# Weighed values through a buffer: VectorE scales them in one product, GpSimd adds them to x

## The chip, the cores and the metric

One core of a Trainium2 chip runs the kernel. The time is that of the device, in microseconds (us), the median of the runs. The engines run side by side and meet through semaphores: TensorE (PE; its weight loads PEld), VectorE (DVE), ScalarE (ACT), GpSimd (POOL), and SyncE (SP), which issues the transfers. Each engine works its own instructions in the order in which they were written.

## The reference, cut to what matters

x has 8 sequences of 512 tokens of 128 numbers. It goes through a routed feed-forward layer, an attention with 16 heads, and the same feed-forward layer again; each adds to x. The change lies in the attention alone:

```python
s = jnp.einsum('bihd,bjhd->bhij', qr, jnp.conj(kr)).real
maha = jnp.maximum(qn[..., None] + (E * E)[None] * kn[:, :, None, :] - 2.0 * E[None] * s, 0.0) / V[None]
logits = coef * jnp.log1p(maha / nu[None, :, None, None]) - 0.5 * DH_ * jnp.log(V)[None]
logits = jnp.where(causal[None, None], logits, -jnp.inf)
A = jax.nn.softmax(logits, axis=-1)
out = jnp.einsum('bhij,bjhd->bihd', A.astype(v.dtype), v)
y = jnp.concatenate([out.real.reshape(B_, N_, DKt), out.imag.reshape(B_, N_, DKt)], axis=-1)
return y @ Wo          # and x = x + this
```

E is a decay exp(-mu |t - t'|) of each head, V depends on it, qn and kn are the squared norms of queries and keys. The kernel multiplies the values by Wo beforehand, so that each head and sequence adds a matrix of 512 tokens by 128 numbers straight to x.

## The kernel before

x stays in SBUF for the whole run (`x_sb`, 128 partitions, 32 tiles of 128x128; a sequence has four). The first feed-forward layer ends near 260 us, the attention near 1476, the second feed-forward layer at the end.

The attention makes 128 pairs of a head and a sequence, in one long row of steps. Head h takes the eight sequences, then head h + 1. The values of two heads are projected together, under the first of the two, which is called even: `values` runs in eight steps (an even octet) and not in the next eight (an odd octet). `PAIRS` is 128, `i` counts pairs of heads and `r` the step in it.

In a step for pair r the engines work on several pairs at once:

- TensorE, in this order: the scores of pair r into the PSUM tile `pS` (L1191), norms of r + 1 (L1204, L82), the projection of r + 2 into `pQK` (L72 to L74), the turn of the probabilities of r - 1 in `pS` (L1233), under even heads the values of r, and `weigh` of r - 2: the probabilities times the values into the PSUM tile `p7` (L1311).
- VectorE: `peaks` of r - 1 (L1578: logarithm plus table, both in SBUF, and the minimum of each row, four pieces of 128, 384, 512 and 256 columns), half of `accumulate` of r - 3 (L1609), `distances` of r (L1587 and the two decay products L1591, out of `pS`), the transpose of the query norms of r + 1 (L1597), the other half of `accumulate`, the rotation's sine and cosine products of r + 2 out of `pQK` (L1631, L1633), the reciprocal of the row sums of r - 1 (L1601). In some steps under even heads it builds the next heads' tables (L1537 to L1567) ahead of the next peaks.
- ScalarE: the exponentials of r - 1 (`soften`, L1376), key norms, clamps, the copy of the turned probabilities, logarithms, squares, and under even heads the values out of PSUM.
- GpSimd: `rotate` of r + 1 (L1500), four products `ek` of decay and key norms (L1509), the query norms `qnorm` (L1517).
- SP: two transfers of the sine product of r + 2, whose halves change places (`crossed`); rotate waits for them.

`accumulate` makes, for each of the four tiles of a sequence, x = p7 * rinv + x, where rinv is the reciprocal of the row sums. Its last product signals `acc_done`; the next `weigh` waits for that before it writes into `p7`. For the last head's eight sequences `moments` follows on VectorE: it waits for `acc_done` and takes mean and variance of the new x (L1618, L1622) for the second feed-forward layer. This is in steps 123 to 130, and the last steps have more work of that layer's head between (variance, refinement, routing).

Of the kernel before, what the change touches and what calls it, by code (L numbers as in the profile page):

```python
# [24 lines left out]
ALU = mybir.AluOpType  # L25
# [3 lines left out]
P = 128  # L29
D = 128  # L30
B, N = 8, 512
TILES = N // P
# [15 lines left out]
SW = 1280  # L48
# [9 lines left out]
def wait(eng, sem, value):  # L58

    if not (isinstance(value, int) and value <= 0):  # L60
        eng.wait_ge(sem, value)
# [981 lines left out]
def attention_phase(nc, s):  # L1043
# [4 lines left out]
    with ExitStack() as ctx:  # L1048
        sb = lambda name, shape, dt=F32: ctx.enter_context(nc.sbuf_tensor(name, shape, dt))
# [7 lines left out]
        decay2, wqk_raw, by_cos, by_sin, crossed = s.decay2, s.wqk_raw, s.by_cos, s.by_sin, s.crossed  # L1057
        squares, rot, knorm, u, z = s.squares, s.rot, s.knorm, s.u, s.z
        qnorm = sb("qnorm", [P, 2, TILES])
        q_turned = sb("q_turned", [P, 2, P])  # L1060
        ek = sb("ek", [P, SW])
        probT = [sb(f"probT{k}", [P, SW]) for k in range(2)]

# [4 lines left out]
        rinv = sb("rinv", [P, 4, TILES])  # L1068
        stats = sb("stats_at", [P, TILES, 6])
        S = s.S  # L1070
# [18 lines left out]
        def hp(h, k):  # L1089

            return s.params[:, h, k:k + 1]
# [16 lines left out]
        def live(i, r):  # L1108

            return not isinstance(i, int) or 0 <= i * 16 + r < PAIRS  # L1110

        def parity(r):

            return (r // B) % 2

        def values_made(i, r):

            return i * B + (r // 16) * B + (r % B + 1 if parity(r) == 0 else B)
# [66 lines left out]
        def _(pe):  # L1185
# [114 lines left out]
            def weigh(i, r):  # L1300
                n = i * 16 + r
                if n == 0:
                    pe.wait_ge(S["late_lo"], 2)
                wait(pe, S["trc_done"], n + 1)
                wait(pe, S["acc_done"], n)
                wait(pe, S["val_done"], values_made(i, r))
                val = val_even[r % B % 3] if parity(r) == 0 else val_odd[r % B]
                turned = probT[r % 2]
                for I in range(TILES):
                    for J in range(I + 1):  # L1310
                        last = pe.matmul(s.p7[:, I * P:(I + 1) * P], turned[:, OFF[I] + J * P:OFF[I] + (J + 1) * P],  # L1311
                                         val[:, J * P:(J + 1) * P], start=(J == 0), stop=(J == I))
                last.then_inc(S["av_done"], 1)
# [175 lines left out]
        def _(g):  # L1489
# [22 lines left out]
            def query_norms(i, r):  # L1512
                n, h = i * 16 + r, i * 2 + r // B
                wait(g, S["qt_done"], n + 1)
                wait(g, S["relu_done"], 2 * (n - 1))
                column = q_turned[:, r % 2].rearrange("p (c d) -> p c d", c=TILES)[:, :, 0]
                g.tensor_scalar(qnorm[:, r % 2, :], column, hp(h, NEG_NU_A), None, ALU.subtract).then_inc(S["qn_done"], 1)  # L1517

            def a_step(i, r):
                if live(i, r + 1):  # L1520
                    if (i, r) != (0, -1):
                        rotate(i, r + 1)
                    spread(i, r + 1)
                    query_norms(i, r + 1)
                if i == 0 and r == -1:
                    build_first()

# [3 lines left out]
        def _(v):  # L1531
# [68 lines left out]
                v.wait_ge(S["exp_done"], i * 16 + r + 1)  # L1600
                v.reciprocal(rinv[:, r % 4, :], rsum[:, r % 4, :]).then_inc(S["rinv_done"], 1)  # L1601

            def accumulate(i, r, tiles=range(TILES)):
                n, b = i * 16 + r, r % B
                v.wait_ge(S["av_done"], n + 1)
                v.wait_ge(S["rinv_done"], n + 1)
                for I in tiles:
                    xt = s.x_sb[:, b * TILES + I, :]
                    last = v.scalar_tensor_tensor(xt, s.p7[:, I * P:(I + 1) * P], rinv[:, r % 4, I:I + 1], xt,  # L1609
                                                  ALU.mult, ALU.add)  # L1610
                if TILES - 1 in tiles:
                    last.then_inc(S["acc_done"], 1)

            def moments(r, n):
                b = r % B
# [117 lines left out]
            def a_step(i, r):  # L1733
                n = i * 16 + r
                if n == PAIRS:
                    accumulate(i, r - 3)
                if live(i, r - 1):
                    peaks(i, r - 1)
                if i == 0 and r in (1, 2):
                    late_low(r - 1)  # L1740
                if live(i, r):
                    if live(i, r - 3):
                        accumulate(i, r - 3, range(TILES // 2))
                    distances(i, r)
                if n == PAIRS - 1:
                    head_low(0)
                    head_low(1)
                if live(i, r + 1):
                    query_norms(i, r + 1)
                if live(i, r - 3) and n != PAIRS:  # L1750
                    accumulate(i, r - 3, range(TILES // 2 if live(i, r) else 0, TILES))
                if n == PAIRS:
                    head_gap()
                    head_first()
# [35 lines left out]
def program(nc, args, out):  # L1790
    with ExitStack() as ctx:
        sb = lambda name, shape, dt=F32: ctx.enter_context(nc.sbuf_tensor(name, shape, dt))
        ps = lambda name, shape: ctx.enter_context(nc.psum_tensor(name, shape, F32))
        s = Shared(args, out)
# [21 lines left out]
        def part(n):  # L1816
# [12 lines left out]
        names = ("w_in trig_in0 trig_in1 w_hi w_lo hp_done arg_done decay_done decay2_done lnv_done lam0_done "  # L1829
                 "lam_done qk_done bs_done crossed_in cos_done sq_done rot_done norm_done q2_done qn_done kn_done "  # L1830
                 "ek_done s_done w_done t_done relu_done ln_done zred_done exp_done v_done "
                 "qt_done val_done tr_done trc_done av_done rinv_done acc_done stat_done dve_passed pool_passed sp_passed "
                 "late_stat late_mv late_var late_ln late_root late_rstd late_step late_xn late_xt late_hi late_lo mv_done expanded0 expanded1")
        s.S = {n: ctx.enter_context(nc.semaphore(n)) for n in names.split()}
        names = ("guw_done silu_done var_done ln_done root_done rstd_done xn_dve xt_done xhi_done xlo_done "
# [12 lines left out]
        s.silu1 = part(2 * N).rearrange("p (a t) -> p a t", a=2)  # L1848
        dense_phase(nc, s, 0)
        attention_phase(nc, s)  # L1850
        dense_phase(nc, s, 1)

# [46 lines left out]
```

## Time and profile before

| | |
|---|---|
| median of 3 runs | 1686.73 us (1685.27 to 1687.78) |
| the profiled execution | 1685.38 us, span 1683.6 |
| PE busy | 1624.1 us, 96% |
| DVE busy | 1494.5 us, 89% |
| ACT busy | 1443.1 us, 86% |
| POOL busy | 1013.6 us, 60% |
| granted TensorE clock | 0.999 |

The span runs from the first to the last instruction that the profile shows. Busy shares are over the whole span, and so mix the three phases. In rows of the timeline, the first number is the start in us from the span's start, the second the duration in us; xN at the end says how many instructions were merged into the row, and a bracket names idle time before it and what ended it. Successive instructions of VectorE overlap by some 0.07 us in these rows, so what one costs is read from start to start.

### The profile page before, as it was taken

Reading aid. Unit: us, or ns where it says so; the run is one execution under the profiler, and the core shown is the slowest. Engines: PE = TensorE matmul, PEld = TensorE weight load, DVE = VectorE, ACT = ScalarE, POOL = GpSimd, SP = SyncE. Lnnn points to the kernel's source line nnn. Section 1 sums busy time; section 2 is a strip of 40 time slices with the busy share of each in tenths; the row PEclk is TensorE's granted clock in tenths of the full one; section 3 lists DMA queues with packets and bytes.
Section 4 is the critical chain, followed back from the end, with each engine's and each line's share of the span. In section 5 each row is a group of like instructions: output and inputs, shape, how many; then the busy total and the mean of one; then the engine's idle time right before and its main releaser. Section 6 shows DMA issues by size and latency. Waiting matters only on the chain. (4 is left out here: it accounts for less than half of the span.)

```text
span 1683.6 us, 31247 instructions
## 1 busy us (share of the span) xinstructions
PE 1624.1 (96%) x9690; PEld 1227.8 (73%) x9690; DVE 1494.5 (89%) x3380; ACT 1443.1 (86%) x2909; POOL 1013.6 (60%) x954
## 2 busy tenths in 40 slices
PE   5999988999999999999999999999999999899998
PEld 4787865777776777677777777777776776677876
DVE  6878878999999999999999999999999989977665
ACT  6677678999999999999999999999999998765765
POOL 3564556666666666665766666666666656245555
PEclk9999999999999999999999999999999999999999
DMA  6000022232223323232222323232232322100000
GB/s 178 1 1 1 1 97 73 64 92 64 76 70 76 79 64 85 58 82 70 75 74 64 92 64 76 55 92 69 74 84 60 80 59 51 26 8 7 13 13 13
DMA packets 50484, 100.05 MB, mean 59 GB/s; under 512 B 8208, under 2 KB 25872, under 8 KB 50320
## 3 DMA queue, kind: packets, MB, share of 16 engines
q1 hardware_dynamic: 50320, 98.07, 22.7%
q8 instruction: 78, 1.28, 0.3%
q14 instruction: 86, 0.70, 0.1%
HBM read 17.95 MB, written 5.24 MB: 14 GB/s over the span
## 5 line engine op out<-in xcount | busy, mean ns | idle before, releaser
L1500 POOL TENSOR_TENSOR early<-early 128x1024 f32<-128x1024 f32 x127 | 303.7, 2391 | 421.4 <-PE pS L1191 227.6
L661 POOL TENSOR_TENSOR hid_lo_d<-hid_d,hid_hi_d 128x512 fp32r<-128x512 f32 x176 | 231.4, 1315 | 218.4 <-ACT hid_hi_d L566 211.8
L1392 ACT ACTIVATE early<-early,qnorm 128x128 f32<-128x128 f32 (+3 forms) x512 | 246.6, 552 | 68.0 <-DVE early L1591 67.3
L1191 PE MATMUL pS<-early 128*128 128x128 f32 (+3 forms) x1024 | 297.6, 433 | 0.4 <-PEq L115 0.4
L1376 ACT ACTIVATE early<-early,nmax 128x128 f32<-128x128 f32 (+3 forms) x512 | 280.9, 558 | 7.7 <-DVE nmax L1578 7.4
L1191 PEld LDWEIGHTS pS<-early 128*128 128x128 f32 x1024 | 164.7, 191 | 96.1 <-issue 61.4
L1587 DVE SCALAR_TENSOR_TENSOR pS<-pS,ek 128x1280 f32<-128x1280 f32 x128 | 190.9, 1492 | 43.5 <-PE pS L1191 41.9
L1509 POOL TENSOR_TENSOR ek<-early 128x128 f32<-128x128 f32 (+3 forms) x256 | 216.1, 877 | 3.0 <-ACT early L1384 2.6
L1509 POOL TENSOR_TENSOR ek<-decay,early 128x128 f32<-128x128 f32 (+3 forms) x256 | 215.0, 873 | 0.0
L1233 PE MATMUL pS<-ident,early 128*128 128x128 f32 x1280 | 184.9, 278 | 13.3 <-DVE early L1591 7.0
L1405 ACT ACTIVATE early<-early,params 128x512 f32<-128x512 f32 (+1 forms) x256 | 196.4, 816 | 0.0
L1233 PEld LDWEIGHTS pS<-ident,early 128*128 128x128 f32 x1280 | 143.5, 141 | 62.1 <-DVE early L1591 32.1
L566 ACT ACTIVATE hid_hi_d<-hid_d 128x512 fp32r<-128x512 f32 x176 | 111.1, 631 | 60.8 <-DVE hid_d L794 43.0
L1399 ACT ACTIVATE probT<-pS 128x1280 f32<-128x1280 f32 x128 | 155.9, 1218 | 3.4 <-PE pS L1233 3.4
L1311 PE MATMUL p<-val_odd,probT 128*128 128x128 f32 x1280 | 156.9, 278 | 1.3 <-ACT probT L1399 1.3
L1311 PE MATMUL p<-val_even,probT 128*128 128x128 f32 x1280 | 154.4, 276 | 0.0
L1311 PEld LDWEIGHTS p<-val_odd,probT 128*128 128x128 f32 x1280 | 147.9, 192 | 6.0 <-ACT probT L1399 1.6
L1609 DVE SCALAR_TENSOR_TENSOR x_sb<-p,rinv,x_sb 128x128 f32<-128x128 f32 x512 | 149.4, 332 | 1.3 <-PE p L1311 1.3
L1311 PEld LDWEIGHTS p<-val_even,probT 128*128 128x128 f32 x1280 | 148.1, 192 | 1.5
L1578 DVE CUSTOM_DVE_ANT_0 early<-early,lam,params 128x128 f32<-128x128 f32 (+3 forms) x256 | 133.6, 575 | 8.8 <-issue 0.5
L1204 PE MATMUL pV<-early,ones 128*128 128x512 f32 x254 | 131.1, 598 | 4.4 <-ACT val_odd L1418 3.9
L1411 ACT ACTIVATE early<-pQK 128x1024 f32<-128x1024 f32 x127 | 127.6, 1005 | 1.8 <-DVE early L1633 1.8
(393 smaller groups left out, 3752.5 us busy)
## 6 DMA issues: line engine op xcount, KB each, us to landing
early<-early SPq DMA_DIRECT2D x263, 256.0 KB, 3.4
early<-trig_d SPq DMA_DIRECT2D x64, 64.0 KB, 2.0
trig_d<-early SPq DMA_DIRECT2D x3, 1024.0 KB, 6.9
early<-in_w SPq DMA_DIRECT2D x3, 704.0 KB, 8.7
x_sb<-in_x SPq DMA_DIRECT2D x4, 512.0 KB, 8.3
early<-in_wqk SPq DMA_DIRECT2D x16, 128.0 KB, 3.4
cos<-trig_d SPq DMA_DIRECT2D x32, 64.0 KB, 2.2
sin<-trig_d SPq DMA_DIRECT2D x32, 64.0 KB, 2.0
```

The lines of the kernel that those rows point to most:

```text
L661: g.tensor_tensor(hid_lo[:, par], hid[:, par], hid_hi[:, par].bitcast(F32), ALU.subtract).then_inc(lo_done, 1)
L1191: last = pe.matmul(s.pS[:, span(I)], rot[:, I * P:(I + 1) * P], rot[:, N:N + (I + 1) * P], start=True, stop=True)
L1233: last = pe.transpose(s.pS[:, col:col + P], z[:, col:col + P], s.ident[:])
L1311: last = pe.matmul(s.p7[:, I * P:(I + 1) * P], turned[:, OFF[I] + J * P:OFF[I] + (J + 1) * P], val[:, J * P:(J + 1) * P], start=(J == 0), ...
L1376: last = a.activation(z[:, span(I)], z[:, span(I)], ACT.Exp, bias=nmax[:, I:I + 1], scale=-1.0, accum_out=rsum[:, r % 4, I:I + 1])
L1392: last = a.activation(u[:, span(I)], u[:, span(I)], ACT.Relu, bias=qnorm[:, r % 2, I:I + 1])
L1399: a.activation(probT[r % 2][:], s.pS[:, 0:SW], ACT.Copy).then_inc(S["trc_done"], 1)
L1405: a.activation(u[:, half], u[:, half], ACT.Ln, bias=hp(h, U_MIN)).then_inc(S["ln_done"], 1)
L1500: g.tensor_tensor(rot[:], by_cos[:], crossed[:], ALU.add).then_inc(S["rot_done"], 1)
L1509: last = g.tensor_tensor(ek[:, span(I)], decay[par][:, span(I)], knorm[:, 0:(I + 1) * P], ALU.mult)
L1587: v.scalar_tensor_tensor(s.pS[:, 0:SW], s.pS[:, 0:SW], -2.0, ek[:], ALU.mult, ALU.add).then_inc(S["w_done"], 1)
L1609: last = v.scalar_tensor_tensor(xt, s.p7[:, I * P:(I + 1) * P], rinv[:, r % 4, I:I + 1], xt, ALU.mult, ALU.add)
```

## The change

VectorE now scales all four tiles in one product into a new buffer `weighed`, and signals `y_done`; GpSimd adds the buffer to x as the last thing in its step, and signals `acc_done`. `weigh` waits for `y_done`. There is one buffer, so the product waits for the add of the pair before. Under odd heads (and where no values are made) the product stands ahead of the transpose of the query norms, under even heads behind it; no part of it is left ahead of `distances`. `moments` waits for `acc_done` as before. The transposed query norms move into columns of `dist` that nothing else uses by then, to make room for the buffer.

```diff
@@ -1057,7 +1057,8 @@
         decay2, wqk_raw, by_cos, by_sin, crossed = s.decay2, s.wqk_raw, s.by_cos, s.by_sin, s.crossed
         squares, rot, knorm, u, z = s.squares, s.rot, s.knorm, s.u, s.z
         qnorm = sb("qnorm", [P, 2, TILES])
-        q_turned = sb("q_turned", [P, 2, P])
+        q_turned = s.dist[:, 2 * N:SW].rearrange("p (k d) -> p k d", k=2)
+        weighed = sb("weighed", [P, TILES, P])
         ek = sb("ek", [P, SW])
         probT = [sb(f"probT{k}", [P, SW]) for k in range(2)]
 
@@ -1302,7 +1303,7 @@
                 if n == 0:
                     pe.wait_ge(S["late_lo"], 2)
                 wait(pe, S["trc_done"], n + 1)
-                wait(pe, S["acc_done"], n)
+                wait(pe, S["y_done"], n)
                 wait(pe, S["val_done"], values_made(i, r))
                 val = val_even[r % B % 3] if parity(r) == 0 else val_odd[r % B]
                 turned = probT[r % 2]
@@ -1516,12 +1517,20 @@
                 column = q_turned[:, r % 2].rearrange("p (c d) -> p c d", c=TILES)[:, :, 0]
                 g.tensor_scalar(qnorm[:, r % 2, :], column, hp(h, NEG_NU_A), None, ALU.subtract).then_inc(S["qn_done"], 1)
 
+            def accumulate(i, r):
+                n, b = i * 16 + r, r % B
+                g.wait_ge(S["y_done"], n + 1)
+                xb = s.x_sb[:, b * TILES:(b + 1) * TILES, :]
+                g.tensor_tensor(xb, xb, weighed[:], ALU.add).then_inc(S["acc_done"], 1)
+
             def a_step(i, r):
                 if live(i, r + 1):
                     if (i, r) != (0, -1):
                         rotate(i, r + 1)
                     spread(i, r + 1)
                     query_norms(i, r + 1)
+                if live(i, r - 3):
+                    accumulate(i, r - 3)
                 if i == 0 and r == -1:
                     build_first()
 
@@ -1600,16 +1609,13 @@
                 v.wait_ge(S["exp_done"], i * 16 + r + 1)
                 v.reciprocal(rinv[:, r % 4, :], rsum[:, r % 4, :]).then_inc(S["rinv_done"], 1)
 
-            def accumulate(i, r, tiles=range(TILES)):
-                n, b = i * 16 + r, r % B
+            def normalise_out(i, r):
+                n = i * 16 + r
                 v.wait_ge(S["av_done"], n + 1)
                 v.wait_ge(S["rinv_done"], n + 1)
-                for I in tiles:
-                    xt = s.x_sb[:, b * TILES + I, :]
-                    last = v.scalar_tensor_tensor(xt, s.p7[:, I * P:(I + 1) * P], rinv[:, r % 4, I:I + 1], xt,
-                                                  ALU.mult, ALU.add)
-                if TILES - 1 in tiles:
-                    last.then_inc(S["acc_done"], 1)
+                wait(v, S["acc_done"], n)
+                v.tensor_tensor(weighed[:], s.p7.rearrange("p (c d) -> p c d", c=TILES),
+                                rinv[:, r % 4, :].unsqueeze(2).broadcast_to([P, TILES, P]), ALU.mult).then_inc(S["y_done"], 1)
 
             def moments(r, n):
                 b = r % B
@@ -1733,22 +1739,23 @@
             def a_step(i, r):
                 n = i * 16 + r
                 if n == PAIRS:
-                    accumulate(i, r - 3)
+                    normalise_out(i, r - 3)
                 if live(i, r - 1):
                     peaks(i, r - 1)
                 if i == 0 and r in (1, 2):
                     late_low(r - 1)
                 if live(i, r):
-                    if live(i, r - 3):
-                        accumulate(i, r - 3, range(TILES // 2))
                     distances(i, r)
                 if n == PAIRS - 1:
                     head_low(0)
                     head_low(1)
-                if live(i, r + 1):
+                values_next = live(i, r) and parity(r) == 0
+                if live(i, r + 1) and values_next:
                     query_norms(i, r + 1)
                 if live(i, r - 3) and n != PAIRS:
-                    accumulate(i, r - 3, range(TILES // 2 if live(i, r) else 0, TILES))
+                    normalise_out(i, r - 3)
+                if live(i, r + 1) and not values_next:
+                    query_norms(i, r + 1)
                 if n == PAIRS:
                     head_gap()
                     head_first()
@@ -1829,7 +1836,7 @@
         names = ("w_in trig_in0 trig_in1 w_hi w_lo hp_done arg_done decay_done decay2_done lnv_done lam0_done "
                  "lam_done qk_done bs_done crossed_in cos_done sq_done rot_done norm_done q2_done qn_done kn_done "
                  "ek_done s_done w_done t_done relu_done ln_done zred_done exp_done v_done "
-                 "qt_done val_done tr_done trc_done av_done rinv_done acc_done stat_done dve_passed pool_passed sp_passed "
+                 "y_done qt_done val_done tr_done trc_done av_done rinv_done acc_done stat_done dve_passed pool_passed sp_passed "
                  "late_stat late_mv late_var late_ln late_root late_rstd late_step late_xn late_xt late_hi late_lo mv_done expanded0 expanded1")
         s.S = {n: ctx.enter_context(nc.semaphore(n)) for n in names.split()}
         names = ("guw_done silu_done var_done ln_done root_done rstd_done xn_dve xt_done xhi_done xlo_done "
```

## Rows read from the trace of the kernel before

**Rows 1.** Busy us by stretch, six even octets: summed length, then engines.

```profile
sum 473.38, PE 472.35 PEld 365.11 DVE 438.14 ACT 452.57 POOL 288.63; mean PE 78.73 PEld 60.85 DVE 73.02 ACT 75.43 POOL 48.10
```

**Rows 2.** Timeline of PE and DVE: scores and L1587, even, then odd.

```profile
728.19 2.32 PE L1191 MATMUL pS<-early 128*128 128x128 f32 x8
...
730.56 1.50 DVE L1587 SCALAR_TENSOR_TENSOR pS<-pS,ek 128x1280 f32<-128x1280 f32 x1 [0.93 <-PE pS L1191]
...
822.63 2.32 PE L1191 MATMUL pS<-early 128*128 128x128 f32 x8
```

**Rows 3.** Busy times by stretch: seven odd octets, sum.

```profile
sum 494.09, PE 487.01 PEld 347.97 DVE 483.89 ACT 456.58 POOL 338.21; mean PE 69.57 PEld 49.71 DVE 69.13 ACT 65.23 POOL 48.32
```

**Rows 4.** Timeline of DVE: one undisturbed step under an odd head.

```profile
816.44 1.48 DVE L1587 SCALAR_TENSOR_TENSOR pS<-pS,ek 128x1280 f32<-128x1280 f32 x1
817.96 1.55 DVE L1591 TENSOR_TENSOR early<-pS,decay 128x512 f32<-128x512 f32 x2
819.43 0.30 DVE L1597 STREAM_TRANSPOSE q_turned<-pV 128x128 f32<-128x128 f32 x1
819.66 0.57 DVE L1609 SCALAR_TENSOR_TENSOR x_sb<-p,rinv,x_sb 128x128 f32<-128x128 f32 x2
820.14 1.21 DVE L1631 TENSOR_TENSOR early<-pQK,sin 128x1024 f32<-128x1024 f32 x1
...
822.71 0.35 DVE L1578 CUSTOM_DVE_ANT_0 early<-early,lam,params 128x128 f32<-128x128 f32 x1
...
822.99 0.61 DVE L1578 CUSTOM_DVE_ANT_0 early<-early,lam,params 128x384 f32<-128x384 f32 x1
...
824.61 0.60 DVE L1609 SCALAR_TENSOR_TENSOR x_sb<-p,rinv,x_sb 128x128 f32<-128x128 f32 x2
825.13 1.49 DVE L1587 SCALAR_TENSOR_TENSOR pS<-pS,ek 128x1280 f32<-128x1280 f32 x1
```

**Rows 5.** Timeline of POOL and DVE: a first piece of peaks beside ek.

```profile
962.33 1.98 POOL L1509 TENSOR_TENSOR ek<-decay,early 128x512 f32<-128x512 f32 x2
...
963.78 0.67 DVE L1578 CUSTOM_DVE_ANT_0 early<-early,lam,params 128x128 f32<-128x128 f32 x1
...
964.38 0.61 DVE L1578 CUSTOM_DVE_ANT_0 early<-early,lam,params 128x384 f32<-128x384 f32 x1
```

**Rows 6.** DVE and POOL: a second piece of peaks beside ek, qnorm.

```profile
813.83 1.07 DVE L1578 CUSTOM_DVE_ANT_0 early<-early,lam,params 128x384 f32<-128x384 f32 x1
...
814.48 0.59 POOL L1517 TENSOR_SCALAR qnorm<-q_turned,params 128x4 f32<-128x4 f32 x1
```

**Rows 7.** Timeline of POOL: first and last row of an even step.

```profile
730.70 2.38 POOL L1500 TENSOR_TENSOR early<-early 128x1024 f32<-128x1024 f32 x1 [3.87 <-PE pS L1191]
...
736.38 0.30 POOL L1517 TENSOR_SCALAR qnorm<-q_turned,params 128x4 f32<-128x4 f32 x1
```

**Rows 8.** Line L1631: least, median, greatest duration in ns; first and last start.

```profile
L1631 DVE TENSOR_TENSOR early<-pQK,sin x64: 1189/1211/1216, 325.2 to 1439.3; 128x1024 f32<-128x1024 f32 x64
```

**Rows 9.** Groups by line, POOL; behind the count: busy us, mean ns, idle us.

```profile
L661 POOL TENSOR_TENSOR hid_lo_d<-hid_d,hid_hi_d 128x512 fp32r<-128x512 f32 x176 | 231.4, 1315 | 218.4 <-ACT hid_hi_d L566 211.8 <-PE p L74 4.3 <-PE pV L74 2.2
```

**Rows 10.** Timeline of DVE: L1587 starting an even octet's last step.

```profile
779.88 1.50 DVE L1587 SCALAR_TENSOR_TENSOR pS<-pS,ek 128x1280 f32<-128x1280 f32 x1 [0.26 <-PE pS L1191]
```

**Rows 11.** Timeline of DVE and POOL: the tail, steps 123, 124 and 128.

```profile
1418.55 0.87 DVE L1618 BATCH_NORM_STATS2 stats_at<-x_sb 128x6 f32<-128x128 f32 x4
...
1419.75 1.19 DVE L1631 TENSOR_TENSOR early<-pQK,sin 128x1024 f32<-128x1024 f32 x1
...
1421.01 0.29 POOL L1517 TENSOR_SCALAR qnorm<-q_turned,params 128x4 f32<-128x4 f32 x1
...
1424.46 1.49 DVE L1587 SCALAR_TENSOR_TENSOR pS<-pS,ek 128x1280 f32<-128x1280 f32 x1
...
1425.31 2.38 POOL L1500 TENSOR_TENSOR early<-early 128x1024 f32<-128x1024 f32 x1 [4.01 <-DMA early<-early]
...
1462.74 1.13 DVE L1609 SCALAR_TENSOR_TENSOR x_sb<-p,rinv,x_sb 128x128 f32<-128x128 f32 x4 [1.34 <-PE p L1311]
```

## The prediction

> **What bounds the kernel now.** I read the busy shares of the page first (TensorE 96%, VectorE 89%, ScalarE 86%, GpSimd 60%): three engines close together, so an average decides nothing. Then I cut the attention phase at the starts of the decay's first product (L1587) into octets of eight steps. A step is one sequence under one head; octets alternate, because `values` runs only under even heads.
>
> Even octets: six take 473.38 us, 9.86 a step, and TensorE is busy for 472.35 of it [rows 1]. VectorE's L1587 starts where the score products end (728.19 + 2.32 = 730.51, start 730.56), after 0.93 of idling [rows 2]. TensorE bounds them.
>
> Odd octets: seven take 494.09, 8.82 a step, VectorE busy for 483.89 [rows 3]. In the timeline of an undisturbed odd step VectorE's instructions stand end to end from one L1587 to the next, 816.44 to 825.13 = 8.69 [rows 4]. The scores end at 822.63 + 2.32 = 824.95 [rows 2]. So VectorE bounds odd steps, with TensorE's floor only 0.13 below (824.95 + 0.05 - 816.44 = 8.56). The other 0.13 of the mean comes from steps in which VectorE is disturbed.
>
> On that disturbance this forecast stands. `peaks` (L1578) reads two SBUF tensors. Its 128x128 form takes 0.35, but 0.67 at 963.78, where GpSimd's ek products still run to 962.33 + 1.98 = 964.31; the next piece starts at 964.38, 0.07 after that end [rows 4, 5]. Its 128x384 form takes 0.61, but 1.07 at 813.83, and GpSimd's 4-element qnorm beside it takes 0.59 instead of 0.30 [rows 4, 6, 7]. Peaks and GpSimd's products keep each other waiting, in both directions. L1631, with one operand in PSUM, shows nothing of the kind: 1189 to 1216 ns over 64 [rows 8].
>
> **VectorE's part of the change.** Removed: four products of 128x128 from PSUM, two before L1587 (825.13 - 824.61 = 0.52) and two behind the transpose (820.14 - 819.66 = 0.48): 1.00 a step [rows 4]. Added: one product of 512 columns out of PSUM. The L1591 pair covers 1280 columns in 819.43 - 817.96 = 1.47, so 512 cost 0.59; the upper end is 0.69, a start of 0.10 included. I take 0.60, as the neighbours overlap so: 0.40 less a step. Peaks start 0.12 later (6.39 behind L1587 instead of 822.71 - 816.44 = 6.27), and nothing stands between them and the next L1587. Alone this makes VectorE's odd step 8.29, and TensorE would hold it at 8.56. The new wait on `acc_done` ahead of the product asks for the add of one step earlier, long done. `weigh` now waits for `y_done`: with the product ahead of the transpose in odd steps that comes at 3.6, earlier than the last accumulate before (3.7), so it costs nothing.
>
> **GpSimd's part.** One add of 128x512 from two SBUF tensors. The same shape takes 1.315 elsewhere [rows 9]; I take 1.31. It is queued last, behind rotate, the four ek products and qnorm. These start 0.14 after L1587 (730.70 - 730.56) and end at 736.38 + 0.30 = 736.68, 6.12 after it [rows 2, 7]. So the add runs from 6.12 to 7.43, in idle time of GpSimd's queue: nothing behind it waits. But peaks want to start at 6.39. They find the add running; the second piece starts 0.07 after its end, at 7.50, and the rest takes 824.61 - 822.99 = 1.62 [rows 4, 5]: VectorE is free at 9.12. The bounds of this collision: nothing at all (8.56 a step, a gain), and the add falling between two pieces, so that its whole 1.31 and some 0.2 of handover come on top of 6.39 + 1.90: 9.8.
>
> The copy that feeds rotate moves too: where rotate waits for it, it starts 5.56 behind the sine product (1419.75 to 1425.31) [rows 11]. That product goes from 3.70 (820.14 - 816.44) to 3.82, so the copy lands at 9.38. With a step of T, rotate starts 9.38 - T behind the next L1587, and T = (9.38 - T) + 8.98 gives T = 9.18. As some copies come later (an estimate, from the odd mean's 0.13 over the undisturbed step), I take 9.25. There are 59 odd steps before the tail: 59 x (9.25 - 8.82) = **+25 us**.
>
> The Trainium skill, "SBUF — State Buffer", section "Who interferes with whom", says that a VectorE instruction with two SBUF inputs and a GpSimd instruction that reads SBUF lock each other out for the whole instruction. Taken to the letter, the next piece could start only 0.28 after the GpSimd product's end; the row at 963.78 shows 0.07. By the rule the odd step would be 0.2 longer (the last rival).
>
> Even steps: VectorE has the same collision (7.50 - 6.39 - 0.28 = 0.83 for peaks, up to 1.1 where a table product stands first; I take 1.0). It loses 0.12 and gains 0.52 ahead of L1587. Where it idled 0.9, all this is hidden under TensorE. In the last two steps of an octet VectorE also builds tables and idled 0.26 or less [rows 10]: 0.26 + 0.40 - 1.0 = -0.34 in each. Seven octets: **+4 us** (0 to 10).
>
> **The tail.** In steps 123 to 126 `moments` waits for `acc_done`, which GpSimd now gives. The sine and cosine products, the reciprocal and peaks are queued behind it on VectorE. Moments began at 1418.55; GpSimd's own work of that step ends at 1421.01 + 0.29, and the add with 0.07 for its signal brings 1422.68: 4.13 later [rows 11]. Less the 0.40 saved, and some 0.4 because rotate starts at 0.2 instead of 0.6 after a step of 9.2: +3.3. The late sine product then delays the next rotate (it needs 5.56, and 1424.46 - 1419.75 - 0.52 = 4.19 are left to the next L1587), to 1.4: +4.5 for each of the next two. In the fourth the refinement steps hide this again: +3.3. Together 15.6. In the last four sequences the add follows the product at once: 1.4 of waiting each, against 0.5 saved (four products took 1.13 [rows 11]): +3.4. **+19 us** (10 to 23).
>
> **Sum.** 25 + 4 + 19 = 48. The profiled execution took 1685.4 (span 1683.6 and 1.8 around it), 1.3 under the median of 1686.73. So 1733.4 as profiled, and 1735 as the median.
>
> **Rivals.**
> Port yields: peaks, issued back to back, keep going and the add waits until they are done (qnorm's 0.59 speaks for it, the 1.07 beside it against [rows 6]). It is decided by who goes first at 6.4. Odd steps fall to TensorE's 8.56: 59 x -0.26 = -15, even 0, tail +19: 1690; with the tail's low end 1681. Not slower, at best faster.
> Half block: the add has its operands early and peaks lose only 0.5: odd steps stay at 8.8, even 0, tail 19: 1706. The 0.67 at 963.78, over nearly all of a product's rest, speaks against it.
> Between the pieces: where rotate starts later than 0.27 behind L1587, a peaks piece goes first and the add falls behind it: 9.8 a step, +58, even 8, tail 19: 1771 if in every step. The 1.07 at 813.83 is such a case [rows 6]; a longer step pulls rotate forward again, which speaks against every step.
> Full block: the first piece starts only at the add's end, 0.2 later in 59 odd steps: +12, 1747. The 0.07 speaks against it.
>
> **Chances.** Forecast 0.57 (its own range 1722 to 1748); port yields 0.10; half block 0.11; between the pieces 0.12; full block 0.10. The range 1698 to 1764 leaves out the first rival and the upper part of the third. Some 0.2% (3.4 us) can be told from no change. Faster 0.04 and the same 0.06 both come from the first rival; slower 0.90.
>
> **What would show it.** In the profile after: odd octets near 74 us, even ones near 79; the first piece of peaks near 1.2 instead of 0.35 in most steps, ending with the add; VectorE still without idle time in odd steps, TensorE with some ahead of its turns; the add at 1.3; ahead of the moments 3 to 5 us of VectorE's idle time in four steps, released by GpSimd. Wrong, if peaks keep 0.35 while the add runs, if the new product takes more than 0.7, or if odd octets lie under 70 us.

## The result and the profile after

The changed kernel takes 1731.97 us (median of 4 runs, 1731.3 to 1736.96) against 1686.0 (4 runs, 1684.09 to 1687.78): 1.028 of before, interval 1.0257 to 1.0302. It is slower. Its profiled execution took 1731.3 us, span 1729.5, at a granted clock of 0.993.

The page of the kernel after: span, then busy time of each engine with its share and count.

```profile
span 1729.5 us, 30866 instructions
...
PE 1634.8 (95%) x9690; PEld 1228.5 (71%) x9690; DVE 1551.7 (90%) x2996; ACT 1455.0 (84%) x2909; POOL 1176.1 (68%) x1082
```

VectorE was given 0.4 us less to do in each of 128 steps, and is busy for 57 us more. The groups by line, shapes apart, say where (behind the bar: busy us, mean ns of one, then idle time before and its releaser):

```profile
L1617 DVE TENSOR_TENSOR weighed<-p,rinv 128x512 f32<-128x512 f32 x128 | 85.5, 668 | 1.5 <-PE p L1312 1.5
L1587 DVE CUSTOM_DVE_ANT_0 early<-early,lam,params 128x128 f32<-128x128 f32 x64 | 57.4, 898 | 4.6 <-ACT early L1406 0.6 <-issue 0.4
...
L1524 POOL TENSOR_TENSOR x_sb<-x_sb,weighed 128x512 f32<-128x512 f32 x128 | 167.7, 1310 | 24.5 <-DVE weighed L1617 24.5
```

The new product and the new add cost what they should. Under odd heads the first piece of peaks (now L1587) takes 898 ns on average, where an undisturbed one takes 0.35 us [rows 4]. All pieces of peaks together grew from 287.8 to 349.8 us.

Cut at the starts of the decay's first product (now L1596), as before, the sums of seven odd and of six even octets:

```profile
sum 513.29, PE 488.39 PEld 344.14 DVE 505.93 ACT 464.85 POOL 405.94; mean PE 69.77 PEld 49.16 DVE 72.28 ACT 66.41 POOL 57.99
...
sum 480.08, PE 476.65 PEld 365.51 DVE 468.03 ACT 454.77 POOL 352.98; mean PE 79.44 PEld 60.92 DVE 78.00 ACT 75.79 POOL 58.83
```

They answer to [rows 3] and [rows 1]: seven odd octets 19.2 us longer, six even ones 6.7. VectorE's timeline of one odd step (the answer to [rows 4]), and GpSimd's of the same step:

```profile
831.21 1.49 DVE L1596 SCALAR_TENSOR_TENSOR pS<-pS,ek 128x1280 f32<-128x1280 f32 x1
832.74 1.56 DVE L1600 TENSOR_TENSOR early<-pS,decay 128x512 f32<-128x512 f32 x2
834.21 0.68 DVE L1617 TENSOR_TENSOR weighed<-p,rinv 128x512 f32<-128x512 f32 x1
834.81 0.31 DVE L1606 STREAM_TRANSPOSE dist<-pV 128x128 f32<-128x128 f32 x1
...
837.50 1.23 DVE L1587 CUSTOM_DVE_ANT_0 early<-early,lam,params 128x128 f32<-128x128 f32 x1
...
838.65 0.61 DVE L1587 CUSTOM_DVE_ANT_0 early<-early,lam,params 128x384 f32<-128x384 f32 x1
...
840.27 1.49 DVE L1596 SCALAR_TENSOR_TENSOR pS<-pS,ek 128x1280 f32<-128x1280 f32 x1
```

```profile
831.36 2.40 POOL L1501 TENSOR_TENSOR early<-early 128x1024 f32<-128x1024 f32 x1 [1.03 <-DMA early<-early]
833.71 3.36 POOL L1510 TENSOR_TENSOR ek<-decay,early 128x128 f32<-128x128 f32 x4
837.04 0.30 POOL L1518 TENSOR_SCALAR qnorm<-dist,params 128x4 f32<-128x4 f32 x1
837.30 1.27 POOL L1524 TENSOR_TENSOR x_sb<-x_sb,weighed 128x512 f32<-128x512 f32 x1
```

Read the two side by side. The add starts at 837.30, the first piece of peaks 0.20 later, and the add runs to 838.57. The piece is shown as busy until 838.73, 0.16 longer than the add (the rows of successive pieces overlap by 0.07 or 0.08), and the second one starts at 838.65, 0.08 behind the add's end. The step takes 840.27 - 831.21 = 9.06.

The tail, step 123: VectorE, GpSimd, and one later row of VectorE (the answers to [rows 11]).

```profile
1441.88 1.49 DVE L1596 SCALAR_TENSOR_TENSOR pS<-pS,ek 128x1280 f32<-128x1280 f32 x1
...
1449.67 0.87 DVE L1624 BATCH_NORM_STATS2 stats_at<-x_sb 128x6 f32<-128x128 f32 x4 [3.89 <-POOL x_sb L1524]
...
1455.07 1.49 DVE L1596 SCALAR_TENSOR_TENSOR pS<-pS,ek 128x1280 f32<-128x1280 f32 x1
...
1503.22 0.87 DVE L1624 BATCH_NORM_STATS2 stats_at<-x_sb 128x6 f32<-128x128 f32 x4 [1.39 <-POOL x_sb L1524]
```

```profile
1448.37 1.27 POOL L1524 TENSOR_TENSOR x_sb<-x_sb,weighed 128x512 f32<-128x512 f32 x1
1456.44 2.37 POOL L1501 TENSOR_TENSOR early<-early 128x1024 f32<-128x1024 f32 x1 [6.80 <-DMA early<-early]
```

VectorE stands idle for 3.89 us until GpSimd's queue has reached the add. The table of waits (total us, times, longest) shows what is new over the whole run; the second row is the exponentials of ScalarE waiting for peaks:

```profile
DVE stats_at L1624 <- POOL x_sb L1524: 20.7, 7, 4.7
...
ACT early L1377 <- DVE nmax L1587: 50.1, 78, 4.9
```

From the starts of the decay's first product in both traces, the 45.9 us of span (1683.6 to 1729.5) fall so: 59 odd steps +19.8 (8.83 to 9.17 each), 56 even steps +6.8 (9.86 to 9.98), steps 123 to 126 +14.7, everything behind the last decay product +4.0, the first eight steps +0.5.

### The profile page after: what moved, and what is told of

Same layout as the page of the kernel before. It is cut to its first block and busy times, and to the rows that moved or that the text cites. A ratio compares the mean times of both kernels' runs of the same rounds, so it can differ in the third digit from the quotient of the medians.

```text
span 1729.5 us, 30866 instructions
## 1 busy us (share of the span) xinstructions
PE 1634.8 (95%) x9690; PEld 1228.5 (71%) x9690; DVE 1551.7 (90%) x2996; ACT 1455.0 (84%) x2909; POOL 1176.1 (68%) x1082
## 5 line engine op out<-in xcount | busy, mean ns | idle before, releaser
L1596 DVE SCALAR_TENSOR_TENSOR pS<-pS,ek 128x1280 f32<-128x1280 f32 x128 | 191.2, 1494 | 17.1 <-PE pS L1192 16.0
L1587 DVE CUSTOM_DVE_ANT_0 early<-early,lam,params 128x128 f32<-128x128 f32 (+3 forms) x256 | 183.0, 767 | 4.6 <-ACT early L1406 0.6
L1524 POOL TENSOR_TENSOR x_sb<-x_sb,weighed 128x512 f32<-128x512 f32 x128 | 167.7, 1310 | 24.5 <-DVE weighed L1617 24.5
L1205 PE MATMUL pV<-early,ones 128*128 128x512 f32 x254 | 131.4, 599 | 15.4 <-ACT early L1412 7.0
```

The source lines that it names most:

```text
L1524: g.tensor_tensor(xb, xb, weighed[:], ALU.add).then_inc(S["acc_done"], 1)
L1587: last = v.tensor_tensor_reduce(z[:, span(I)], u[:, span(I)], lam(h)[:, near(I)], hp(h, NEG_COEF), HIGHEST, ALU.add, ALU.min, nmax[:, I:I ...
L1596: v.scalar_tensor_tensor(s.pS[:, 0:SW], s.pS[:, 0:SW], -2.0, ek[:], ALU.mult, ALU.add).then_inc(S["w_done"], 1)
```

## The experiments

Theory: two waits. Peaks, which read two SBUF tensors, and GpSimd's add, which reads two as well, keep each other waiting in every step; and moments wait for an add at the end of GpSimd's queue. The rivals put the cost on the new product, on its place, on the waits (`y_done`, `acc_done`) or on GpSimd's time as such. Each row below has the ratio of the kernel's runs to those of the kernel before, with its interval. The other columns are of the profiled execution and worked out from the starts of the decay's first product: mean of the 59 odd and the 56 even steps, and the length of steps 123 to 126 and of all behind the last, against before.

| kernel | ratio (interval) | odd | even | 123 to 126 | behind |
|---|---|---|---|---|---|
| before | 1 | 8.83 | 9.86 | 0 | 0 |
| after | 1.0279 (1.0257 to 1.0302) | 9.17 | 9.98 | +14.7 | +4.0 |
| no_add | 0.9886 (0.987 to 0.9903) | 8.59 | 9.86 | -1.9 | -1.1 |
| memset2 | 1.0009 (0.9999 to 1.0018) | 8.54 | 9.87 | +14.4 | +2.3 |
| half_add | 1.0068 (1.0053 to 1.0083) | 8.77 | 9.87 | +13.0 | +0.7 |
| between | 1.0138 (1.0122 to 1.0154) | 9.02 | 9.87 | +6.6 | +2.6 |
| tail_old | 1.0167 (1.015 to 1.0184) | 9.23 | 9.98 | 0.0 | +0.1 |
| even_only | 0.9995 (0.9986 to 1.0004) | 8.78 | 9.89 | +0.1 | 0.0 |
| sine_first | 1.0147 (1.0132 to 1.0162) | 9.18 | 9.90 | +1.6 | +0.1 |
| acc_behind | 1.0053 (1.004 to 1.0067) | 8.93 | 9.86 | +2.4 | 0.0 |
| one_ahead | 0.9984 (0.9975 to 0.9993) | 8.77 | 9.86 | +3.1 | 0.0 |

**no_add.** The product stays, GpSimd's add goes (cut from the diff):

```diff
-                wait(pe, S["y_done"], n)
+                wait(pe, S["acc_done"], n)
...
-                if live(i, r - 3):
-                    accumulate(i, r - 3)
...
-                                rinv[:, r % 4, :].unsqueeze(2).broadcast_to([P, TILES, P]), ALU.mult).then_inc(S["y_done"], 1)
+                                rinv[:, r % 4, :].unsqueeze(2).broadcast_to([P, TILES, P]), ALU.mult).then_inc(S["acc_done"], 1)
```

> GpSimd's add is left out (the attention's result is not added to x); VectorE's product signals acc_done itself. Theory (peaks and the add exclude each other, and moments wait for the add): odd steps fall from 9.17 to TensorE's 8.56, the first piece of peaks is back near 0.35, tail and even octets lose their excess: 1670 (1664 to 1678). Rival (VectorE's new product or its place costs the time): odd steps stay above 8.9, over 1700.

Measured: 1666.24 us, inside the range. Seven odd octets, and the first piece of peaks:

```profile
sum 480.61, PE 477.24 PEld 347.16 DVE 471.24 ACT 455.11 POOL 339.69; mean PE 68.18 PEld 49.59 DVE 67.32 ACT 65.02 POOL 48.53
```

```profile
L1585 DVE CUSTOM_DVE_ANT_0 early<-early,lam,params 128x128 f32<-128x128 f32 x64 | 32.9, 514 | 4.0 <-issue 0.4
```

VectorE's part alone would be worth 19.6 us of 1685.84. The whole loss, and more, comes with the add; the product, its place and the moved query norms are all still in this kernel. The piece's 514 instead of 410 ns before is what ek alone does to it in a shorter step.

**memset2.** The same place in GpSimd's queue and the same waits, but two fills of `weighed` that only write, in place of the add that reads:

```diff
-                g.tensor_tensor(xb, xb, weighed[:], ALU.add).then_inc(S["acc_done"], 1)
+                g.memset(weighed[:], 0.0).then_inc(S["set_done"], 1)
+                g.wait_ge(S["set_done"], n + 1)
+                g.memset(weighed[:], 0.0).then_inc(S["acc_done"], 1)
```

> In place of the add GpSimd writes zeros over the buffer, twice, one after the other (x gets nothing): it is busy at the same place of its queue and signals from there, but reads nothing. Theory (the two shut each other out over reads from SBUF): the first piece of peaks keeps 0.35 to 0.55 beside it, odd steps stay at the 8.6 measured without an add; the moments still wait for it: 1668 to 1690, by the length of the two writes. Rival (any work of GpSimd at that place, by its queue or by writing to SBUF, costs the 0.6 a step): odd steps 9.0 or more, 1710 to 1735.

Measured: 1687.13, by the theory. The fills, by line, and a step's timeline on VectorE and on GpSimd:

```profile
L1524 POOL MEMSET weighed<- 128x512 f32 x128 | 67.2, 525 | 23.6 <-DVE weighed L1619 23.6
```

```profile
796.79 0.61 DVE L1589 CUSTOM_DVE_ANT_0 early<-early,lam,params 128x384 f32<-128x384 f32 x1
...
797.33 0.74 DVE L1589 CUSTOM_DVE_ANT_0 early<-early,lam,params 128x512 f32<-128x512 f32 x1
```

```profile
796.97 0.52 POOL L1524 MEMSET weighed<- 128x512 f32 x1
797.55 0.53 POOL L1526 MEMSET weighed<- 128x512 f32 x1
```

Peaks run through the fills at their own 0.61 and 0.74. GpSimd is busy for 1.1 us of the end of the step all the same (525 + 560 ns), and odd steps take 8.54: neither GpSimd's time nor the waits, but its reading, makes odd steps long. The tail keeps +14.4: there it is the place in the queue alone. The two parts of the cost come apart, and the tail by itself eats what 59 odd steps save.

The Trainium skill, "SBUF — State Buffer", section "Who interferes with whom", says that a VectorE instruction with two SBUF inputs contends with a GpSimd instruction that reads SBUF, and not with one that only writes it. These rows agree: 1.23 for the piece beside the add, 0.61 and 0.74 beside the fills.

**half_add.** The add over two of the four tiles:

```diff
-                g.tensor_tensor(xb, xb, weighed[:], ALU.add).then_inc(S["acc_done"], 1)
+                g.tensor_tensor(xb[:, 0:2], xb[:, 0:2], weighed[:, 0:2], ALU.add).then_inc(S["acc_done"], 1)
```

> The add takes two of the four tiles (the other two are left out): 0.74 us instead of 1.31 by the ek product of 256 columns. Theory (peaks wait as long as the add has to go): odd steps 8.8 to 8.9, even octets without excess, tail 0.57 shorter in eight places: 1704 (1696 to 1712). Rival (a price of each meeting, whatever its length): odd steps 9.1, 1722 to 1730.

Measured: 1697.25, inside the range. The add takes 828 ns instead of 1310 (0.74 us had been expected), and odd steps take 8.77, which is 0.40 less for 0.48 less of reading; even steps are back at 9.87. The less GpSimd reads at that place, the less it costs.

**between.** The add of the pair before, with operands long there, in the middle of the four ek products:

```diff
                 for I in ORDER:
+                    if I == ORDER[2] and live(i, r - 4):
+                        accumulate(i, r - 4)
...
-                if live(i, r - 3):
+                if live(i, r - 3) and not live(i, r + 1):
                     accumulate(i, r - 3)
```

> The add is queued between the second and the third ek product instead of last; nothing else changes. Theory (GpSimd's 7.36 of reading and the 1.9 of peaks can't overlap, so that 9.2 a step is due wherever the add stands): odd steps 9.1 to 9.3 as before, now with ek and qnorm beside peaks; the moments wait 2.2 less in four steps: 1723 (1715 to 1732). Rival (the add only stands at the wrong place): odd steps 8.6 to 8.7, 1696 (1690 to 1702).

Measured: 1709.7, between the two expectations, so both were wrong. One odd step of that kernel, GpSimd and VectorE:

```profile
683.50 1.28 POOL L1526 TENSOR_TENSOR x_sb<-x_sb,weighed 128x512 f32<-128x512 f32 x1
684.74 2.02 POOL L1512 TENSOR_TENSOR ek<-decay,early 128x512 f32<-128x512 f32 x2
686.74 0.60 POOL L1520 TENSOR_SCALAR qnorm<-dist,params 128x4 f32<-128x4 f32 x1
```

```profile
685.82 0.36 DVE L1589 CUSTOM_DVE_ANT_0 early<-early,lam,params 128x128 f32<-128x128 f32 x1
...
686.11 1.07 DVE L1589 CUSTOM_DVE_ANT_0 early<-early,lam,params 128x384 f32<-128x384 f32 x1
```

With the add out of the way, the later ek products meet peaks. Here the first piece comes just behind the border of two ek products (684.74 + 1.01 = 685.75) and keeps its 0.36; only the second waits, for the last product. This step took 8.65; steps in which rotate had started over 1.5 us behind the decay product took 9.7 to 10.2. So place matters in part, and my sentence that the step is 9.2 wherever the add stands does not hold. The tail's excess falls from 14.7 to 6.6, since the add no longer comes last.

**tail_old.** From step 123 on VectorE accumulates as before; all else as after. (Some 30 lines choose the way by the step's number; core:)

```diff
+            def new_way(i, r):
+                # of the step in which the pair's values are added
+                n = i * 16 + r
+                return n < (H - 1) * B + 3
...
+                    if new:
+                        normalise_out(i, r - 3)
+                    else:
+                        accumulate(i, r - 3, range(TILES // 2 if live(i, r) else 0, TILES))
```

> The last eight pairs, those with moments, are added by VectorE as before the change; all others go through the buffer. Theory: the excess of the tail (14.7 in steps 123 to 126 and 4.0 behind them) goes, all else stays: 1713 (1710 to 1717). Rival (the tail is only where a delay from before comes out): 1726 or more.

Measured: 1714.12, inside the range. The tail is back to within 0.1 us and no wait of VectorE for GpSimd's add is left, while odd steps stay long, at 9.23. So the two waits come apart: 1731.97 - 1714.12 = 17.9 us go with the tail and what is behind it, where the traces had 14.7 + 4.0 = 18.7. (In the two traces the odd steps differ as well, 9.17 and 9.23, or 3.8 us over 59; why was not looked into.)

**even_only.** The same switch, the new way only in steps r = 0 to 4 under even heads (37 adds in the trace, two of them in the first octet):

```diff
+                return n < (H - 1) * B + 3 and parity(r) == 0 and r % B < 5
```

> Only steps 0 to 4 of the even octets go through the buffer, all others as before. Theory (there the collision is the same, 0.8 on VectorE, and hidden under TensorE's 9.86): 1686 (1684 to 1690), with pieces of peaks stretched in these steps. Rival (each add costs, wherever it is): 35 adds at 0.36, the mean price of an add (46 us for 128), 1698.

Measured: 1685.45, no change. A collision in such a step: the third piece of peaks takes 1.75 instead of 0.74, and VectorE still idles 0.57 ahead of the decay's first product (L1609 in this kernel).

```profile
566.31 1.75 DVE L1600 CUSTOM_DVE_ANT_0 early<-early,params 128x512 f32<-128x512 f32 x1
...
569.04 1.50 DVE L1609 SCALAR_TENSOR_TENSOR pS<-pS,ek 128x1280 f32<-128x1280 f32 x1 [0.57 <-PE pS L1200]
```

Where TensorE bounds the step and VectorE idles ahead of that product, the collision is nearly free: in the trace the 56 even steps are 1.4 us longer in all, which the odd steps, 2.9 us shorter here, cover in the total.

The last three kernels go back to the one before and ask whether the gain that no_add shows can be had without GpSimd.

**sine_first.** In odd steps the sine product goes ahead of the transpose, and all four accumulate products ahead of `distances`:

```diff
-                        accumulate(i, r - 3, range(TILES // 2))
+                        accumulate(i, r - 3, range(TILES if early else TILES // 2))
                     distances(i, r)
...
+                if early:
+                    turn_sine(i, r + 2)
...
-                if live(i, r - 3) and n != PAIRS:
+                if live(i, r - 3) and n != PAIRS and not early:
```

> The kernel before the change, but in odd steps VectorE makes the sine product straight behind distances, and all four accumulate products ahead of them; GpSimd adds nothing. If it is the late start of rotate that brings ek beside peaks, rotate starts 0.7 earlier, at 0.14 in most steps, and odd steps come to their undisturbed 8.69 to 8.72: 59 x -0.12 = -7, 1679 (1676 to 1682). Rival (the 0.13 of the mean has another cause, or TensorE waits for the later transpose or distances): 1686 or more.

Measured: 1710.21, a miss by 31 us. The collisions are gone, as meant: the first piece takes 0.35 in odd steps. But the step is 9.22. VectorE and ScalarE in one:

```profile
829.34 1.49 DVE L1587 SCALAR_TENSOR_TENSOR pS<-pS,ek 128x1280 f32<-128x1280 f32 x1
...
835.62 0.35 DVE L1578 CUSTOM_DVE_ANT_0 early<-early,lam,params 128x128 f32<-128x128 f32 x1 [0.66 <-ACT early L1405]
...
838.55 1.49 DVE L1587 SCALAR_TENSOR_TENSOR pS<-pS,ek 128x1280 f32<-128x1280 f32 x1
```

```profile
833.48 1.22 ACT L1399 ACTIVATE probT<-pS 128x1280 f32<-128x1280 f32 x1
834.60 1.54 ACT L1405 ACTIVATE early<-early,params 128x512 f32<-128x512 f32 x2
```

Peaks wait 0.66 for ScalarE's logarithms and start 6.28 behind L1587. In [rows 4] they start 6.27 behind it, although VectorE had other work ahead of them there. In the kernel after it is 6.29, with again other work ahead. Two more rows of the step of [rows 4], VectorE's last one ahead of peaks and ScalarE's logarithms:

```profile
822.41 0.17 DVE L1601 RECIPROCAL rinv<-rsum 128x4 f32<-128x4 f32 x1
```

```profile
821.69 1.53 ACT L1405 ACTIVATE early<-early,params 128x512 f32<-128x512 f32 x2
```

Peaks start 0.13 behind the end of the reciprocal there, where successive instructions of VectorE otherwise overlap, and 822.71 - 821.69 = 1.02 behind the start of the logarithms; in sine_first it is 835.62 - 834.60 = 1.02 as well. So they waited for the logarithms before the change too, only too briefly to stand out. A loop over two engines was hidden in those rows: decay products, clamps, the copy of the turned probabilities, logarithms (6.28 to the start of peaks), and peaks themselves (837.51 - 835.62 = 1.89 for the four pieces): 8.17 at least. Every product between peaks and L1587 comes on top: two (0.52) gave 8.69, four (1.04) give 9.21. "VectorE's instructions end to end" was the wrong reading; the length agreed.

**acc_behind.** With the loop in mind: nothing between peaks and L1587, all four products behind `distances`, ahead of the sine product:

```diff
-                    if live(i, r - 3):
+                    if live(i, r - 3) and not early:
                         accumulate(i, r - 3, range(TILES // 2))
...
+                if early:
+                    accumulate(i, r - 3)
+                    turn_sine(i, r + 2)
...
-                if live(i, r - 3) and n != PAIRS:
+                if live(i, r - 3) and n != PAIRS and not early:
```

> The kernel before the change, but in odd steps all four accumulate products stand straight behind distances, and the sine product behind them; GpSimd adds nothing. In sine_first, peaks waited 0.66 for the logarithms: from L1587 over decay products, clamps, copy and logarithms to peaks and the next L1587 runs a second loop, of 8.17 without accumulate, and whatever stands between peaks and L1587 is added to it (0.52 gave 8.69, 1.04 gave 9.21). If so, odd steps are no longer held by it but by TensorE's 8.45 or VectorE's sum of 8.55; with some ek beside peaks, as rotate starts 0.25 later, 8.60 to 8.70: 59 x -0.17 = -10, 1676 (1672 to 1680). Rival (8.69 is VectorE's own sum, or weigh waits for the later acc_done): 1685 or more.

Measured: 1695.26; the rival held. VectorE's and TensorE's rows of one odd step:

```profile
829.48 1.50 DVE L1587 SCALAR_TENSOR_TENSOR pS<-pS,ek 128x1280 f32<-128x1280 f32 x1 [0.36 <-PE pS L1191]
...
832.49 1.12 DVE L1609 SCALAR_TENSOR_TENSOR x_sb<-p,rinv,x_sb 128x128 f32<-128x128 f32 x4
```

```profile
833.71 2.47 PE L1311 MATMUL p<-val_odd,probT 128*128 128x128 f32 x20 [0.21 <-issue]
836.01 2.32 PE L1191 MATMUL pS<-early 128*128 128x128 f32 x8
```

`weigh` starts 0.10 behind the end of the last product (833.61), after 0.21 of standing still: it waits for `acc_done`. That closes another loop: 4.13 from L1587 to the end of the last product, 0.10 to `weigh`, 4.62 to the end of the scores (836.01 + 2.32 = 838.33), and 0.05 to the next L1587 as in [rows 2], 8.90 in all. 44 of the 59 odd steps take 8.88 or 8.89. (The one shown takes 9.09, because a piece of peaks is stretched in it.) Here the changed kernel's one product, 0.60 instead of 1.0 long, helps: in no_add most odd steps take 8.45 or 8.46.

**one_ahead.** One product ahead of `distances`, three behind, then the sine product:

```diff
-                        accumulate(i, r - 3, range(TILES // 2))
+                        accumulate(i, r - 3, range(1 if early else TILES // 2))
...
+                if early:
+                    accumulate(i, r - 3, range(1, TILES))
+                    turn_sine(i, r + 2)
...
-                if live(i, r - 3) and n != PAIRS:
+                if live(i, r - 3) and n != PAIRS and not early:
```

> As acc_behind, but one of the four accumulate products stands ahead of distances and three behind: GpSimd adds nothing. In acc_behind a step of 8.89 was held by weigh, which waited 0.21 for acc_done. With three behind, acc_done comes at 3.8 after L1587, about when the turns end, and the loop over ScalarE is 8.17 + 0.26 = 8.43: VectorE's sum of 8.55 should hold odd steps, 8.56 to 8.68 with the stretched pieces of peaks: 59 x -0.2 = -12, 1674 (1670 to 1679). Rival (weigh still waits, or the later sine product brings more ek beside peaks): 1683 or more.

Measured: 1682.74 against 1685.14, ratio 0.9984 (0.9975 to 0.9993). It beats both kernels, the one before by 0.16% only, and lies far from the 1674 expected, just under the rival's 1683: an undisturbed odd step falls from 8.69 to 8.63 only, and steps 123 to 126 lose 3.1.

## Why the prediction came out right

The forecast was 1735 us, the result 1731.97. The profiled span grew by 45.9, with 48 forecast.

- **The product.** 0.60 from start to start (834.81 - 834.21), as taken.
- **Peaks start later.** Not so: 837.50 - 831.21 = 6.29 behind the decay's first product, 6.39 forecast and 6.27 before. They hang on ScalarE's logarithms (sine_first), not on VectorE's sum. It cost the forecast nothing, since the add ends later anyway.
- **The collision.** The add starts 837.30 - 831.21 = 6.09 behind the product (6.12 forecast) and takes 1.27 here; the next piece follows 0.08 behind its end (0.07 forecast), and the rest takes 840.27 - 838.65 = 1.62, as forecast to the digit. That the add as such does this is shown by no_add, that it does so by reading by memset2, and that the reading time sets the size by half_add.
- **Rotate.** 0.15 behind the decay product in the step shown, 0.2 forecast; over the 59 odd steps the median is 0.30, but single steps have it from 2.7 ahead to 1.5 behind.
- **Odd steps: +19.8, forecast +25.** Two terms were off. The six middle steps of an octet take 9.20 on average, where the equation without the estimate gave 9.18: the 0.07 that I added for late copies was not there. And the first odd step of an octet takes 8.85 in six of eight cases, because GpSimd comes out of an even step with rotate started 0.15 ahead of the decay product. I had treated all 59 as settled. They are not: they run from 8.83 to 9.99, and a long and a short one often take turns (9.35, 8.97, 9.34, 8.94 in steps 44 to 47, with rotate at 0.42, 0.04, 0.41 and 0.05). The equation holds that too, since a longer step lets the next rotate start earlier by as much; its 9.18 is then the mean of such a pair. That the mean over all of them comes within 0.02, although in 19 of the 59 the add held up a later piece than the first (see the rivals), is in part luck.
- **Even steps: +6.8, forecast +4.** The last two steps of an octet lose 0.34 and 0.28 (0.34 forecast), in six of the seven octets (but for one last step, below). There the add meets a table instruction, and peaks run undisturbed behind it:

```profile
636.95 1.36 DVE L1553 CAST wqk_hi<-early 128x256 fp32r<-128x256 f32 x1
...
639.10 0.35 DVE L1587 CUSTOM_DVE_ANT_0 early<-early,params 128x128 f32<-128x128 f32 x1
```

```profile
636.89 1.27 POOL L1524 TENSOR_TENSOR x_sb<-x_sb,weighed 128x512 f32<-128x512 f32 x1
```

The cast took 0.26 in the trace of before; beside the add (636.89 + 1.27 = 638.16) it is busy until 638.31, though it has one input. Most of the rest of the 6.8 is one step that I had not foreseen, of 12.67 us instead of 9.86 (VectorE, then GpSimd):

```profile
494.95 2.60 DVE L1587 CUSTOM_DVE_ANT_0 early<-early,dist,params 128x256 f32<-128x256 f32 x1
```

```profile
494.81 2.46 POOL L1501 TENSOR_TENSOR early<-early 128x1024 f32<-128x1024 f32 x1 [2.61 <-PE pS L1192]
```

Rotate starts 0.14 ahead of the last piece, and the piece (0.48 otherwise) waits all of it out. In tail_old the same step took 12.66, and one more like it came up, step 91 with 11.98, under an odd head.
- **The tail: +14.7, forecast +15.6.** Step by step +3.4, +4.2, +4.2, +2.8 against +3.3, +4.5, +4.5, +3.3. The late rotate stands at 1456.44 - 1455.07 = 1.37 behind the decay product (1.4 forecast). tail_old takes the whole away.
- **Behind it: +4.0, forecast +3.4.** Moments wait 1.38 to 1.41 us (1.4 forecast), but three times and not four. What I left out is that the add meets peaks once more there, in the last step.

```profile
1507.09 1.61 DVE L1587 CUSTOM_DVE_ANT_0 early<-early,lam,params 128x384 f32<-128x384 f32 x1
```

- **The rivals.** Port yields: no, the first piece takes over 0.9 in 38 of the 59 odd steps, and the add keeps its 1.26 to 1.31 in 49 (it takes 1.67 at most). Half block: no, the next piece starts only behind the add's end in the step shown. Between the pieces: in 19 odd steps the first piece went ahead of the add, which then held up a later one, but 15 of these took 9.19 to 9.43, not 9.8. Only the five longest odd steps come near that price, 9.65 to 9.99, with rotate over 1.3 behind (or, once, 2.7 ahead). Full block: 0.08 against the 0.28 that it asked for; the add's reading shuts peaks out, but not quite to the end of its record. TensorE's floor of 8.56, on which the first rival stood, was too high, though: without the add undisturbed odd steps ran at 8.45.

The errors partly cancel: odd steps 5 too many, even ones 3 too few, the tail 0.3 too many.

## What to carry to other kernels

Before work goes to an engine that looks idle, look at what the receiving engine's instruction reads, and lay it in time over the giver's instructions that read two SBUF operands: here 0.40 us saved a step cost some 0.9 of standing still (1.23 less 0.35), and a write in the same place cost nothing. A signal that moves to another engine comes only when that engine's queue has got to it, so every waiter of it has to be looked at again; here four steps of 128 paid a third of the loss. Where instructions stand end to end, move one and see whether the next starts earlier before the engine is called the bound: a loop over two engines can have the same length.

## What had not been expected of the hardware

Of peaks and the add: the second piece starts 0.08 behind the add's recorded end, while an undisturbed first piece takes 0.28 from its start to the next one's (822.99 - 822.71 in [rows 4]). So either the first piece did some 0.2 us of its work while the add ran, or the add had stopped reading some 0.2 us before its recorded end; the rows don't show which.

TensorE's clock fell in the tail as a consequence of the wait. Windows of 1 us of the kernel after: length, busy of PE, PEld, DVE, ACT and POOL, the granted clock, then the DMA share and GB/s.

```profile
1450.88:1451.88 1.00, 0.00 (x0) 0.00 (x0) 1.00 (x3) 0.00 (x0) 0.00 (x0) 1.00 0.00 0
...
1453.88:1454.88 1.00, 0.57 (x1) 0.50 (x2) 1.00 (x5) 1.00 (x4) 0.00 (x0) 0.50 0.92 213
...
1459.88:1460.88 1.00, 1.00 (x12) 1.00 (x11) 0.00 (x0) 0.00 (x0) 1.00 (x2) 1.00 0.00 0
```

TensorE stood idle for 4.01 us up to 1454.31, and within that the clock went from 1.00 to 0.50, that is from 2.4 to 1.2 GHz; the window from 1459.88 has 1.00 again, after some 5 us of work. The norms of L1205 took 2.07 us at the lower clock, and 1.12 one step later. In tail_old, without the wait, the clock of steps 123 to 126 is 1.00. The next step (14.05) was bound elsewhere: moments wait for GpSimd's queue (rotate to add, 1456.44 to 1463.62) and begin at 1463.65. Whether the lower clock adds some tenths in the steps behind was not separated.
